# Selective scan with FFN on one core: half of the scan's drives of three batches as scaled tiles turned by PE, in a new instruction order

## The reference

```python
delta = softplus(dt_proj_w @ dt_lo + dt_proj_b)     # 256 channels x 256 steps
A = -exp(A_log)                                     # 256 channels x 16 states
def step(state, xs):
    d_t, B_t, C_t, u_t = xs
    dA = exp(d_t[..., None] * A)
    state = state * dA + (d_t * u_t)[..., None] * B_t[:, None, :]
    y_t = einsum('ben,bn->be', state, C_t)
    return state, y_t
...
y = (y + D * u) * silu(layernorm(x))
x = x + tanh(g_xattn) * y
gate, up = bitlinear(layernorm(x), w_gate), bitlinear(layernorm(x), w_up)
x = x + tanh(g_ffn) * h_bitlinear(silu(gate) * up, w_down)
```

## Time and profile before

| | us |
|---|---|
| median of 3 runs | 214.35 |
| lowest, highest run | 212.56, 214.4 |
| the profiled execution | 211.92 |
| its span, first to last instruction | 210.2 |
| first scan begins, last product with C ends | 23.98, 177.29 |

### The profile page before, as it was taken

One profiled execution on the slowest core, in us unless ns is written; L12 is line 12 of the kernel. 1 busy time (PEld: TensorE's weight loads), 2 busy tenths in 40 slices (PEclk: granted clock), 3 DMA queues, 4 the chain that ended last, 5 costly groups with the idle time before them and its releaser, 6 DMA issues.

```text
span 210.2 us, 3818 instructions
## 1 busy us (share of the span) xinstructions
PE 192.7 (92%) x1314; PEld 160.0 (76%) x1320; DVE 182.2 (87%) x272; ACT 163.1 (78%) x284; POOL 111.2 (53%) x142
## 2 busy tenths in 40 slices
PE   6899899799999998999999999999599899779983
PEld 6789787577889886687899877897486589746962
DVE  1957469999998999999899999999899996779972
ACT  2589999998999879996996996995997211287382
POOL 1047109797831990089999550999800499830000
PEclk9999999999999999999999999999999999999999
DMA  5994000000000000000000000000000000000001
GB/s 132 330 361 142 0 2 2 3 0 0 0 5 0 0 3 2 0 0 3 2 0 3 0 0 25 3 2 25 3 0 0 0 30 25 0 3 0 25 28 50
DMA packets 8148, 6.34 MB, mean 30 GB/s; under 512 B 2202, under 2 KB 7874, under 8 KB 8130
## 3 DMA queue, kind: packets, MB, share of 16 engines
q1 hardware_dynamic: 6898, 6.01, 8.9%
q10 hardware_dynamic: 1232, 0.10, 0.5%
HBM read 5.05 MB, written 1.05 MB: 29 GB/s over the span
## 4 chain that ended last, share of the span: by engine, by line
PE 58%; DVE 14%; POOL 11%; issue 8%; ACT 7%; DVEq 0%; POOLq 0%; ACTq 0%
PE PY L482 10%; PE BC L419 9%; PE UP L419 9%; POOL wnat L1528 4%; PE GP L601 4%; POOL wnat L1529 4%; DVE state L1643 3%; PE GP L632 3%; PE X L360 3%; PE X L511 2%; PE BC L466 2%; PE GP L616 2%; DVE wnat L1812 1%; PE PY L491 1%; PE UP L654 1%
## 5 line engine op out<-in xcount | busy, mean ns | idle before, releaser
L1073 ACT ACTIVATE decay<-delta,zero_c,aneg 128x255 f32<-128x255 f32 x128 | 65.7, 589 | 0.1
L1643 DVE TENSOR_TENSOR_SCAN state<-decay,BC 128x512 f32<-128x512 f32 x32 | 38.7, 1211 | 8.3 <-PE BC L419 7.6
L1528 POOL TENSOR_TENSOR wnat<-wnat 128x512 f32<-128x512 f32 x18 | 23.0, 1275 | 33.7 <-DVE wnat L1764 33.1
L1720 DVE TENSOR_TENSOR prod<-state,BC 128x1024 f32<-128x1024 f32 x32 | 38.5, 1202 | 1.2 <-issue 0.5
L1643 DVE TENSOR_TENSOR_SCAN state<-decay,UP 128x512 f32<-128x512 f32 x32 | 38.5, 1203 | 0.6 <-issue 0.5
L419 PE MATMUL BC<-diagB,duT 128*128 128x256 f32 x128 | 33.7, 385 | 1.8 <-DVE state L1643 1.6
L419 PE MATMUL UP<-diagB,duT 128*128 128x256 f32 x128 | 33.3, 383 | 0.4 <-DVE state L1643 0.4
L482 PE MATMUL PY<-id,prod 128*128 128x128 f32 x256 | 32.6, 273 | 0.0
L482 PEld LDWEIGHTS PY<-id,prod 128*128 128x128 f32 x256 | 29.0, 141 | 1.6 <-DVE prod L1720 0.3
L419 PEld LDWEIGHTS BC<-diagB,duT 128*128 128x128 f32 x128 | 22.3, 190 | 6.0 <-issue 3.5
L419 PEld LDWEIGHTS UP<-diagB,duT 128*128 128x128 f32 x128 | 22.7, 190 | 4.5 <-issue 1.6
(11 more groups left out here) (249 smaller groups left out, 390.1 us busy)
## 6 DMA issues: line engine op xcount, KB each, us to landing
xs<-in_x_dram SPq DMA_DIRECT2D x1, 1024.0 KB, 6.5
wnat<-in_L_ffn_w_gate_dram SPq DMA_DIRECT2D x1, 1024.0 KB, 9.0
wnat<-in_L_ffn_w_up_dram SPq DMA_DIRECT2D x1, 1024.0 KB, 10.9
wnat<-in_L_ffn_w_down_dram SPq DMA_DIRECT2D x1, 1024.0 KB, 11.4
out_dram<-ot SPq DMA_DIRECT2D x8, 128.0 KB, 1.7
ctxs<-in_ctx_dram SPq DMA_DIRECT2D x1, 384.0 KB, 4.1
ctxs<-in_ctx_dram SPq DMA_DIRECT2D x1, 128.0 KB, 2.8
inw<-n_L_xattn_in_proj_w_dram SPq DMA_DIRECT2D x1, 128.0 KB, 2.7
```

The lines of the kernel that those rows point to most:

```text
L1073: last = nc.scalar.activation(decay[:, m % RING, h, n, 1:L], delta[:, b % 2, h, 1:L], ACT.Exp, bias=zero_c[:], scale=aneg[:, h, NB * j + n ...
L1528: nc.gpsimd.tensor_tensor(dst[:, :, 0, :], src[:, :, 0, :], src[:, :, 1, :], ALU.add)
L1643: nc.vector.tensor_tensor_scan(state[:, g % STATES, h].rearrange("p n l -> p (n l)"), decay[:, g % RING, h].rearrange("p n l -> p (n l)"), ...
L1720: nc.vector.tensor_tensor(prod[:, g % RING].rearrange("p h n l -> p h (n l)"), state[:, g % STATES].rearrange("p h n l -> p h (n l)"), PC. ...
```

## The change

Steps of batches 1 to 3 whose states lie in quarters 1 and 3 (m = 10, 11, 14, 15, 18, 19, 22, 23, 26, 27, 30, 31) get their drive in another way. POOL multiplies duT by B with B as a scalar for each partition (the time step): four scalings of 128x256 (two halves of the time, two states), into a tile of a ring of three. Two tiles of the ring lie where the diagonals of quarters 1 and 3 lay; the third is new. PE then turns this tile into the drive's bank with four f32 transposes for each half. The other steps, and all of batch 0, stay as they were; POOL builds two diagonal tiles instead of four for batches 1 to 3. The lists of calls of all four engines are new.

```diff
+SCALED = [m for m in range(B * STEPS) if m >= STEPS and m * NB // PER % 2 == 1]
+DRIVE_RING = 3
...
+        driveT = [diagB[:, q].rearrange("p c (n h) l -> p c n (h l)", n=NB) for q in (1, 3)] + [sb("driveT", [P, LC, NB, E])]
...
+
+        def diagonals_by(b, q):
+
+            return q + 1 if b == 0 else QUARTERS + (b - 1) * QUARTERS // 2 + q // 2 + 1
...
                 pe.wait_ge(act_duT, b + 1)
-                pe.wait_ge(pool_diagB, m * NB // PER + 1)
+                q, at = divmod(NB * j, PER)
+                if m in SCALED:
+                    pe.wait_ge(pool_scaled, SCALED.index(m) + 1)
+                else:
+                    pe.wait_ge(pool_diagB, diagonals_by(b, q))
                 if m >= 1:
                     pe.wait_ge(dve_scan, HALF * (m - 1) + h + 1)
                 else:
                     pe.wait_ge(act_setup, (2, 3)[h])
-                q, at = divmod(NB * j, PER)
-                for c in range(LC):
-                    last = nc.tensor.matmul(drive_bank(h).rearrange("p (n c l) -> p n c l", n=NB, c=LC)[:, :, c, :],
-                                            duT[:, b % 2, c, P * h:P * (h + 1)], diagB[:, q, c, at:at + NB, :],
-                                            start=True, stop=True)
+                if m in SCALED:
+                    for n in range(NB):
+                        for c in range(LC):
+                            last = nc.tensor.transpose(drive_bank(h)[:, L * n + P * c:L * n + P * (c + 1)],
+                                                       driveT[SCALED.index(m) % DRIVE_RING][:, c, n, P * h:P * (h + 1)],
+                                                       id32[:])
+                else:
+                    for c in range(LC):
+                        last = nc.tensor.matmul(drive_bank(h).rearrange("p (n c l) -> p n c l", n=NB, c=LC)[:, :, c, :],
+                                                duT[:, b % 2, c, P * h:P * (h + 1)], diagB[:, q, c, at:at + NB, :],
+                                                start=True, stop=True)
                 last.then_inc(pe_drive, 1)
 
...
-                    act.wait_ge(pool_diagB, QUARTERS * (n - 1))
+                    act.wait_ge(pool_diagB, diagonals_by(n - 2, QUARTERS - 1))
+                if n >= 3:
+                    act.wait_ge(pool_scaled, STEPS // 2 * (n - 2))
...
+            def scaled(m):
+
+                b, j = divmod(m, STEPS)
+                k = SCALED.index(m)
+                pool.wait_ge(act_BT, b + 1)
+                pool.wait_ge(act_duT, b + 1)
+                if k >= DRIVE_RING:
+                    pool.wait_ge(pe_drive, HALF * (SCALED[k - DRIVE_RING] + 1))
+                elif k < 2:
+                    pool.wait_ge(pe_drive, HALF * STEPS * (k + 1) // 2)
+                q, at = divmod(NB * j, PER)
+                for c in range(LC):
+                    for n in range(NB):
+                        last = nc.gpsimd.tensor_scalar(driveT[k % DRIVE_RING][:, c, n], duT[:, b % 2, c],
+                                                       BT[:, b % 2, q, c, at + n:at + n + 1], 1.0, ALU.mult, ALU.mult)
+                last.then_inc(pool_scaled, 1)
+
...
             drive_rows(0, 1)
-            x_dbl(1)
             drive_rows(1, 0)
             drive_rows(1, 1)
+            gate_T(0)
+            C_rows(0)
...
```

More of the change, by code:

```diff
@@ L867, in _ @@
             drive_rows(15, 0)
-            up(0, 1)
-            drive_rows(15, 1)
-            accumulate(11)
-            C_rows(14)
-            accumulate(12)
-            drive_rows(16, 0)
+            gate(0, 1)
+            C_rows(14)
+            drive_rows(15, 1)
+            up(0, 0)
+            drive_rows(16, 0)
+            accumulate(12)
+            up(0, 1)
+            drive_rows(16, 1)
             C_rows(15)
-            drive_rows(16, 1)
+            dt_proj(3)
+            drive_rows(17, 0)
@@ new lines, in _ @@
+            drive_rows(22, 1)
+            q2_T(0, 0)
+            C_rows(21)
+            drive_rows(23, 0)
+            gate(1, 1)
+            accumulate(20)
+            drive_rows(23, 1)
+            up(1, 0)
+            C_rows(22)
+            drive_rows(24, 0)
+            down(0, 0)
+            drive_rows(24, 1)
+            q2_T(0, 1)
+            gate_T(3)
+            C_rows(23)
+            drive_rows(25, 0)
+            up(1, 1)
+            drive_rows(25, 1)
+            accumulate(21)
@@ L1280, in _ @@
             decays(1, 0)
+            decays(1, 1)
+            decays(2, 0)
             for_silu()
+            silu_z(0)
+            silu_u(1)
             tanh_gates()
-            silu_u(1)
-            silu_z(0)
             for_exp()
+            gate_out(0)
+            decays(2, 1)
             dt_rows(1)
-            decays(1, 1)
             copy_BT(1)
-            decays(2, 0)
-            decays(2, 1)
             high_pieces(1)
@@ L1335, in _ @@
             decays(15, 0)
+            decays(15, 1)
             for_silu()
+            silu_u(3)
             tokens_out_early(0)
-            conv_out(3)
-            silu_u(3)
+            copy_duT(2)
+            silu_z(2)
             silu_gate(0, 0)
-            silu_z(2)
-            copy_duT(2)
+            dt_rows(3)
+            copy_BT(3)
+            high_pieces(3)
             silu_gate(0, 1)
             for_exp()
-            decays(15, 1)
             decays(16, 0)
-            dt_rows(3)
-            copy_BT(3)
             decays(16, 1)
             decays(17, 0)
+            spread(3)
             decays(17, 1)
-            high_pieces(3)
+            softplus(3)
             decays(18, 0)
@@ L2037, in _ @@
             times_C(31)
+            absmax2(2, 0)
             last_residual()
```

393 lines of the change are left out of this document (188 added, 205 removed).

## The result

| | kernel before | changed kernel |
|---|---|---|
| median, us | 213.45 | 216.19 |
| ratio, 95% interval | | 1.0157 (1.0108 to 1.0206) |
| first scan begins, us | 23.98 | 24.93 |
| first scan to scan (8, 0) | 33.16 | 36.30 |
| scan (8, 0) to the end of the last product | 120.15 | 119.65 |

What follows compares the result with a forecast made beforehand. DVE was taken as the bound, idle only 7.87 of 153.31 us. Gains of 0.5 (batch 0) and 3.85 (batches 1 to 3) less 0.95 (tail) made 3.4 us off 214.35, forecast 211.0, range 208.8 to 214.8.

Steps and rivals of the forecast that it cites:

- The place of pick_rows: Batch 0, DVE: its copies, moved between scan (0, 0) and scan (0, 1), were to take 0.7 us there.
- a price on GpSimd's sets of at most 0.7 us: GpSimd: a scaled set beside a two-port DVE operation would cost up to 0.7 us more, within the slack.
- the walk through batch 0: Front and batch 0: first norm hidden by DVE, scan (8, 0) at about 56.6 instead of 57.14; 0.5 us gained.
- rival 3: Batch 0: ACT waits at silu_z for a late r1 from DVE's first norm; 2.5 us lost, 213.5 us; chance 0.04.
- 3.85 of the 4.71 us: Batches 1 to 3: shorter, earlier drives close 3.85 us of DVE's 4.71 us of waits; 0.85 stay.
- a slack of 1.2 us: GpSimd at du of batch 3: 1.2 us left before scan (22, 0), so a set may cost 2.1 us.
- My lower end for this term: Batches 1 to 3: a gain of only 1.5 us if new waits of the old size come at other places.
- the move costs 0.95 us: Tail: hadamard (2, 0) ahead of accumulate (31) on PE makes the residual start 3.4 us earlier instead of 4.35.
- rival 2: GpSimd bounds at du of batch 3, slower kernel: decides from 3.0 us a set, 215.6 at 3.3; chance 0.10.
- 10.1: PE: 24 scaled drives at 0.44 us instead of 0.86 take 10.1 us off its busy time.
- rival 4: Batch 3: PE's clock falls to its lower level for 10 us, losing 5 us, 216 us; chance 0.04.

Runs made afterwards that it cites:

- e2: Changed kernel plus eight filler products of 128 x 128 ones on PE between drive(1,0) and drive(1,1), where PE waits for scan(0,1); 214.65 us.
- e8: Changed kernel plus one wait: GpSimd begins diagonals(0,1) and (0,2) only after DVE's pick_rows casts, which stay between the two scans; 212.78 us.
- e11: Changed kernel with pick_rows back, du of batch 3 earlier on GpSimd, and the tail's calls on PE, DVE and ACT put back as before; 210.71 us.
- e1: Changed kernel with one call moved: pick_rows back between inw_taps() and first_conv() on DVE, as in the kernel before; 212.67 us.
- e10: e1 with GpSimd's du of batch 3 (last part of its softplus tail) moved ahead of token_factors(1) and diagonals(3,0); 212.14 us.
- e14: e11 with every drive made by diagonal products again, so no scaled drives; 214.66 us.
- e9: e1 with two tail calls back: accumulate(31) ahead of hadamard(2,0) on PE, absmax2(2,0) behind the residual and statistics on DVE; 215.16 us.

## Why the prediction was wrong

From a gain of 3.4 us to a loss of 4.3 in the profiles are 7.7 us: 3.64 of them lie in batch 0, 3.35 in batches 1 to 3 and 0.95 ahead of the first scan, and the tail came 0.24 better than forecast.

**The place of pick_rows.** The step that failed is "The two copies of pick_rows (0.22 + 0.53) now stand between scan (0, 0) and scan (0, 1): 0.7 us". With GpSimd's diagonals beside them they cost 1.7 us more than in the same place without (34.64 in e2, 32.91 in e8), and through PE's clock another 1.7 (36.30 in the change, 34.64 in e2). Their durations came from a row in which GpSimd did nothing; their new place had the diagonals of batch 0 beside them. The Trainium skill ("SBUF — State Buffer", section "Who interferes with whom") says that when DVE runs in a 2-port mode, as casts and tensor_scalar operations (the roundings here) can, whichever of DVE and GpSimd issues first has the shared ports for its whole instruction, and the other is blocked. I had read it from one side, as a price on GpSimd's sets of at most 0.7 us, and never asked which short DVE operations now fall beside GpSimd. The traces agree with the rule on both sides: 0.18 to 1.04 us for a cast, 0.68 to 1.78 for a rounding, and 1.27 to 1.77 for GpSimd's product where DVE went first. The rest of the walk through batch 0 was right: without the lock (e11) scan (8, 0) begins at 56.65, forecast 56.6, and with the casts in the place that was forecast (e8) it comes 32.91 us behind the first scan, forecast 32.6; DVE's first norm was hidden, and the late r1 of rival 3 cost nothing: ACT begins silu_z (0) at 26.39 in e1 without a wait.

**Batches 1 to 3.** "So 3.85 of the 4.71 us close" failed too, and not because of batch 0: with that mended (e1) the stretch is 119.75, a gain of 0.40. Two causes were taken apart. GpSimd gives du of batch 3 behind token_factors (1) and diagonals (3, 0), and the product of step 21 and a scan of step 22 waited; putting it earlier gave 1.16 us (e10). I had left a slack of 1.2 us there, with du at 119.8. In e1 it ended at 121.09: GpSimd's queue from scaled (18) to du took 36.4 us, forecast 36.1, but began at 84.69, where I had the copy of duT end at 83.7. So the slack was used up. In the changed kernel, 3.55 us late at scan (16, 0) once the FFN product that the change moved behind it is counted, du ended at 125.47. And a rounding and a cast of DVE fall beside GpSimd, which is busy without a pause there: 1.1 us each time. It happened once in each profile of this order with scaled drives, twice in e7, and not at all in the kernel before and in e14. In e11 the gain is 1.52. By its windows DVE is busy for 115.94 us and idle for 2.69, where 115.45 and 0.85 had been forecast: 0.49 and 1.84 short, together 2.33. Of the idle time DVE's waits name these as the largest:

```profile
DVE amax L1789 <- ACT xn L1196: 0.9, 2, 0.5
DVE state L1685 <- issue: 0.4, 1, 0.4
```

The token maximum waits for ACT's second norm twice, 0.9 us; no such wait was over 0.2 before. Which of the moved calls makes it was not tried. The rest is small waits at many places. My lower end for this term, 1.5 (new waits of the old size at other places), is where it came out once du was moved; as the change stood, with 0.50, it fell below that end.

**The tail.** "So the move costs 0.95 us": the residual comes 3.15 us behind the last product instead of 2.24, 0.91 later, and the stretch is 0.71 longer. Right, though not all of it reaches the end of the span: with the tail back as a whole the stretch is 0.42 shorter (33.54 in e10, 33.12 in e11). That the move hangs together with a third call on ACT I had not seen; e9 showed it.

**GpSimd and PE.** 1.91 us a set against 1.84, 126.7 busy against 126.3; rival 2 (3 us a set) is out. PE gives back 7.8 us in the middle stretch (114.83 in e14, 107.00 in e11), where 10.1 had been forecast, 0.33 a drive instead of 0.42; why it is less is open. As most of it is idle time of PE either way, that term weighed little.

**PE's clock.** It fell, as in rival 4, but after a wait and in batch 0, where there are no scaled drives. In the stretch of the scaled drives it is 1.00 in the changed kernel and in e1, e10 and e11. The Trainium skill ("TensorE: Matmul & The Clock Gate", "Part 4: PE-mode transpose") says that transposes do not count as busy for the clock in the way that other products do; a loss from that, in a stretch where half of the drives and all accumulates are transposes, no run here shows.

So the idea was sound and the size too large: the whole change, without the two faults of its order and with the tail of before, gives 1.0% (e11), of which the scaled drives carry 2.8 us in batches 1 to 3 (e14). As it was made, one call in front of the second scan is what lies between no change (e1, 0.9991) and a loss of 1.6%.

## What to carry to other kernels

A duration read where GpSimd is idle need not hold beside GpSimd: when a change moves a short cast or rounding of DVE, list what GpSimd issues at that time and count that operation's whole length once for each cast it can catch. When a wait is put in front of PE, price not only the wait but also the clock behind it: here a wait of 2.47 us drew 1.7 us more. Calls that release each other across engines (here a maximum on DVE, a scaling on ACT and a product on PE) are moved together or not at all.
